# Weight rows of a graph layer: unrelated columns summed from adjacency bytes, and two of eight head additions through GpSimd

## The reference

```python
h = relu(layernorm(x))
q = (h[sub] @ Wq.T + bq), k = (h[obj] @ Wk.T + bk)      # 8 heads of 64, 10000 pairs (sub, obj) below 1500
scores[:, sub, obj] = (q * k).sum(-1) / 8               # elsewhere 0
scores = where(adj, scores, -inf); scores[:, i, i] = 1e-7
x = x + (softmax(scores, axis=2).sum(heads) / 8) @ h
```

## Time and profile before

| what | value |
|---|---|
| median of 3 runs | 1131.22 us (1126.92 to 1132.14) |
| profiled execution | 1126.64 us, its span 1124.9 us |
| PE, DVE, ACT, POOL busy | 1050.8, 917.9, 786.5, 277.0 us |
| L743, float32 products of W with h | 384 records, 184.9 us |
| L1185, additions of a head | 96, 170.8 us, 1.779 each |
| L1196, masks | 96, 161.1 us, 1.715 each |

### The profile page before, as it was taken

The page is one execution under the profiler, slowest core; times in us unless marked ns, Lnnn a source line. Parts: engine busy times, 40 slices in busy tenths (PEclk is TensorE's granted clock), DMA queues, the critical chain, the costliest instruction groups (busy, mean ns, idle before and its releaser), DMA issues. The chain is left out here.

```text
span 1124.9 us, 25112 instructions
## 1 busy us (share of the span) xinstructions
PE 1050.8 (93%) x10560; PEld 715.8 (64%) x10565; DVE 917.9 (82%) x1259; ACT 786.5 (70%) x833; POOL 277.0 (25%) x272
## 2 busy tenths in 40 slices
PE   1999997999999999999988599999999999999997
PEld 1444443444444444444444499999999999999743
DVE  2355146899999999999981899999999999999466
ACT  1244336777777777776633799999999999998122
POOL 2778750000000000000000244334344344434000
PEclk9999998999999999999999799999999999999999
DMA  9640443322212221100054587767777777777311
GB/s 336 162 29 2 114 91 77 79 68 68 66 40 41 68 59 59 38 20 29 23 215 155 156 196 186 183 171 180 183 187 183 191 203 180 181 182 184 122 69 75
DMA packets 71552, 136.45 MB, mean 121 GB/s; under 512 B 9237, under 2 KB 18834, under 8 KB 69394
## 3 DMA queue, kind: packets, MB, share of 16 engines
q1 hardware_dynamic: 50386, 101.19, 25.7%
q0 software_dynamic: 21056, 33.67, 20.4%
HBM read 92.92 MB, written 25.04 MB: 105 GB/s over the span
## 5 line engine op out<-in xcount | busy, mean ns | idle before, releaser
L1511 ACT ACTIVATE area_h<-area_a,keep 128x2048 fp8e4<-128x2048 f32 x197 | 376.8, 1989 | 4.2 <-PE psum L1666 4.1
L1665 PE MATMUL psum<-s_V,area_h 128*128 128x99 bf16 x3072 | 298.1, 209 | 0.8 <-DVE area_b L1437 0.5
L1665 PEld LDWEIGHTS psum<-s_V,area_h 128*128 128x128 fp8e4 x3072 | 283.4, 98 | 1.1 <-DVE area_h L1561 0.7
L1666 PE MATMUL psum<-s_V,area_b 128*128 128x99 bf16 x2048 | 204.1, 209 | 0.0
L1666 PEld LDWEIGHTS psum<-s_V,area_b 128*128 128x128 fp8e4 x2048 | 189.5, 97 | 0.0
L743 PE MATMUL psum<-area_h,f_region 128*128 128x512 f32 x384 | 184.9, 596 | 0.0
L1185 DVE SCALAR_TENSOR_TENSOR f_region<-area_b,s_r,f_region 128x1500 f32<-128x1500 f32 x96 | 170.8, 1779 | 2.2
L1561 DVE TENSOR_TENSOR area_h<-area_h,area_a 128x512 uint32<-128x512 uint32 x256 | 167.9, 686 | 4.4
L1196 DVE CUSTOM_DVE_ANT_0 area_b<-psum,late 128x1500 f32<-128x1500 f32 x96 | 161.1, 1715 | 8.2 <-PE psum L658 8.1
L1668 PE MATMUL psum<-s_V,area_h 128*128 128x198 bf16 x1024 | 150.0, 249 | 13.7 <-DVE area_h L1561 13.7
L977 ACT ACTIVATE area_b<-area_b,s_negm 128x1500 f32<-128x1500 f32 x96 | 147.8, 1540 | 20.9 <-DVE s_negm L1196 19.9
(11 more groups left out here) (185 smaller groups left out, 1423.0 us busy)
## 6 DMA issues: line engine op xcount, KB each, us to landing
area_a<-s_rows SPq DMA_DIRECT2D x16, 1024.0 KB, 7.2
late<-area_h POOLq DMA_DIRECT2D x64, 256.0 KB, 4.4
late<-far_rows SPq DMA_DIRECT2D x60, 256.0 KB, 4.1
area_b<-area_h POOLq DMA_DIRECT2D x48, 256.0 KB, 4.6
area_b<-far_rows SPq DMA_DIRECT2D x45, 256.0 KB, 3.5
rel_planes<-f_h SPq DMA_DIRECT2D x3, 2304.0 KB, 15.9
late<-rel_planes SPq DMA_DIRECT2D x36, 192.0 KB, 2.6
area_h<-in_x SPq DMA_DIRECT2D x4, 1024.0 KB, 12.9
```

Of the source, the lines that this page charges most:

```text
L1511: act.activation(masks[:, j, :], s1b[:, b, :], ACT.Relu, bias=t["s2"][:, n, 0, j:j + 1], scale=BIG, saturate=False).then_inc(signs, 1)
L1665: pe.matmul(out[:, :, 0:DZ], masks[:, j, cols], V[:, b, j, :, 0:DZ], **first)
L1666: last = pe.matmul(out[:, :, DZ:CZ], fars[FAR.index(j)][:, cols], V[:, b, j, :, DZ:CZ], **then)
```

## The change

In short: for related row tiles the columns of the four unrelated tiles (1536 to 2047) no longer go through W. W has 1536 columns; its aggregation has six rounds of two tiles for eight. The sum over the four far tiles is made by PE as in `gather`, from a transposed chunk of adjacency bytes (`far_chunk`, reloaded from DRAM by SP, `load_far`) and kept bf16 parts, twelve products of 512 columns (`sum_far`, `unrelated`). VectorE scales that sum late, with half of c0 as bytes are 2, while adding it to x (`finish_far`). It shares PSUM bank 7 with the sum of W, so the first product of W waits for `finish_far`.

Second, heads 5 and 7 of tiles 0 to 10 are no longer added to W by VectorE. ScalarE scales their exponentials by the ratio of the two heads' factors (`weigh`), GpSimd adds them to heads 4 and 6 (`merge`), and VectorE adds heads 4 and 6 when that is done. The last tile adds all eight.

To make room, small tables of the first stage lie in another buffer, the projected rows have one store buffer for two, and the marked relations lie in their own plane, for which its reload waits longer.

The core of the diff:

```diff
+MERGED = ((4, 5), (6, 7))
@@ bank_rounds
-        order += turns(n, 5) + [quarter[2]] + turns(n, 6) + [quarter[3]] + turns(n, 7) + [("h", n + 2)]
+        order += turns(n, 5) + [quarter[2], quarter[3], ("h", n + 2)]
@@ stage2, SP
+            def load_far(i):
+                k = NU - 1 + i
+                sp.wait_ge(chunk_out[place(k)], 16 * (stored(k) + 1))
+                if i:
+                    sp.wait_ge(far_in, 16 * i)
+                if i >= 2:
+                    sp.wait_ge(far_summed, i - 1)
...
+                sp.dma_start(f.far_chunk[i % 2], t["adj_chunks"][tile_at(k)][:, ET * P:].rearrange("p (j i) -> p j i", j=4)
+                             ).then_inc(far_in, 16)
@@ POOL
+            def merge(n, i):
+                into, source = MERGED[i]
+                pool.wait_ge(weighed, len(MERGED) * n + i + 1)
+                pool.wait_ge(added, added_until(n, 2 * (i + 1)))
+                pool.tensor_tensor(ex[:, into, 0:NREL], ex[:, into, 0:NREL], ex[:, source, 0:NREL], ALU.add).then_inc(merged, 1)
@@ PE
+            def sum_far(i, bank, alone):
+                pe.wait_ge(far_in, 16 * (i + 1))
...
+                for b in range(NT - ET):
+                    moving = (f.upper(h[:, ET + b, :]), f.far_rest[b // 2][:, b % 2, :], f.far_tail[b])
+                    for part in range(3):
...
+                        last = pe.matmul(ps[:, bank, :], f.far_chunk[i % 2][:, b, :], moving[part],
+                                         start=alone and first, stop=alone and final)
+                last.then_inc(far_summed, 1)
@@ aggregate
-                if m == order[0] and r < ET - 1:
-                    pe.wait_ge(*((summed, NU + r) if r else (based, NU)))
+                if m == 0 and blocks[0] == 0 and r < ET - 2:
+                    pe.wait_ge(based, NU + r + 1)
@@ step (PE)
                 if scored:
                     score(n + 1, 0)
+                if turned:
+                    unrelated(r)
                 project(n + 1)
@@ ACT
             def start_w(r):
...
+                act.activation(half[:, r % 2:r % 2 + 1], cd[:, 0:1], ACT.Copy, scale=1.0 / NEAR).then_inc(w_started, 1)
+                act.activation(W[r % 2][:, :], adjn[:, (r + NU) % ADJ_RING, 0:NE], ACT.Copy, scale=cd[:, 0:1]).then_inc(w_started, 1)
+            def weigh(r):
+                act.wait_ge(fac, LINKS * (r + 1))
+                for i, (_, source) in enumerate(MERGED):
+                    act.activation(ex[:, source, 0:NREL], ex[:, source, 0:NREL], ACT.Copy, scale=ratio[:, i:i + 1]).then_inc(weighed, 1)
@@ step (ACT)
                 start_w(n)
+                weigh(n)
@@ DVE
+            def finish_far(r):
+                k = r + NU
+                dve.wait_ge(far_summed, r + 2)
...
+                dve.scalar_tensor_tensor(xt[k % 3][:, :], ps[:, far_bank(r), :], half[:, r % 2:r % 2 + 1], xt[k % 3][:, :],
+                                         ALU.mult, ALU.add).then_inc(based, 1)
@@ factors
+                dve.tensor_tensor(ratio[:, :], z[:, 4:HA:2], rz[:, 5:HA:2], ALU.mult).then_inc(fac, 1)
@@ step (DVE)
                 for p in range(PAIRS):
                     for hd in (2 * p, 2 * p + 1):
-                        add_head(n, hd)
+                        if hd in adds(n):
+                            add_head(n, hd)
+                    if p == 0 and n:
+                        finish_far(n - 1)
                     for hd in (2 * p, 2 * p + 1):
                         if n + 1 < ET:
                             mask(n + 1, hd)
```

More of the change, by code:

```diff
@@ L493, in stage2 @@
     cd = sb("cd", [P, 2])
+    half = sb("half", [P, 2])
+    ratio = sb("ratio", [P, len(MERGED)])
     stats = sb("stats", [P, 6])
@@ L500, in stage2 @@
     chunk_out = [sem(f"chunk_out{i}") for i in range(3)]
-    seq_out = [sem(f"seq_out{i}") for i in range(2)]
+    seq_out = sem("seq_out")
     wseq_in, a_in = sem("wseq_in"), sem("a_in")
@@ L526, in stored, with adds, added_until, far_bank @@
         return sum(place(x) == place(k) for x in ORDER[:ORDER.index(k)])
+    def adds(r):
+        return tuple(hd for hd in range(HA) if r == ET - 1 or hd not in [source for _, source in MERGED])
+    def added_until(r, count):
+        return sum(len(adds(x)) - 1 for x in range(r)) + count
+    def far_bank(r):
+        return 7 if r < ET - 2 else r - ET + 3
     def turned_round(r, m):
@@ L639, in _ @@
             pool.wait_ge(f.rel_in[0], 16 * PLANES)
-            for k in range(NU + 3, NT):
+            for k in range(NU + 3, NU + ADJ_RING):
                 load_adj(k)
-            pool.wait_ge(w_started, ET)
+            for n in range(ET - 1):
+                if n + NU + ADJ_RING < NT:
+                    load_adj(n + NU + ADJ_RING)
+                merge(n, 0)
+                merge(n, 1)
+            pool.wait_ge(w_started, 2 * ET)
             heads.gpsimd(pool)
@@ L743, in aggregate @@
                     last = pe.matmul(ps[:, 7 if r < ET - 1 else 0, :], WT[m % 2][:, b, :], h[:, 2 * m + b, :],
-                                     start=(m == order[0] and b == 0), stop=(m == order[-1] and b == 1))
+                                     start=(m == 0 and b == 0), stop=(m == AG - 1 and b == 1))
                 if blocks[-1] == 1:
@@ L865, in last_steps @@
                 turn_one_and_scores(ET - 1)
-                for m in range(2, 7):
+                for m in range(2, AG):
                     turn_w(r, m)
@@ L1111, in _, with keep_parts @@
         def _(dve):
+            def keep_parts():
+                dve.wait_ge(f.proj, GROUPS)
+                dve.wait_ge(f.parted, 2 * NT)
+                for i in range(2):
+                    upper = f.rest[:, ET + 2 * i:ET + 2 * i + 2, :].bitcast(BF16).rearrange("p t (c w) -> p t c w", w=2)[:, :, :, 1]
+                    dve.tensor_copy(f.far_rest[i], upper).then_inc(f.parted, 1)
+                dve.tensor_copy(f.far_tails, f.tail[:, ET:ET + 2, :]).then_inc(f.parted, 1)
+                for b in (2, 3):
+                    dve.tensor_copy(f.far_tail[b], f.tail[:, ET + b, :]).then_inc(f.parted, 1)
             def score_weights():
@@ L1183, in add_head @@
                 w = W[r % 2][:, 0:NREL]
-                dve.wait_ge(*((added, (HA - 1) * r + hd) if hd else (diag_added, r + 1)))
+                dve.wait_ge(*((added, added_until(r, adds(r).index(hd))) if hd else (diag_added, r + 1)))
+                for i, (into, source) in enumerate(MERGED):
+                    if hd == into and source not in adds(r):
+                        dve.wait_ge(merged, len(MERGED) * r + i + 1)
                 dve.scalar_tensor_tensor(w, ex[:, hd, 0:NREL], r8[:, hd:hd + 1], w, ALU.mult, ALU.add
-                                         ).then_inc(added if hd < HA - 1 else w_ready, 1)
+                                         ).then_inc(added if hd < adds(r)[-1] else w_ready, 1)
             def mask(r, hd):
```

197 lines of the change are left out of this document (111 added, 86 removed).

## The result

The changed kernel takes 1140.75 us (median of four runs, 1139.75 to 1142.16) against 1129.17 us before in the same series: a ratio of 1.0098, 95% interval 1.0067 to 1.0129. Forecast were 1140.6. The profiled execution took 1141.06 us, its span is 1139.3.

A forecast was written before the change was run, and what follows sets the result against it. VectorE's own list was taken as the bound, with TensorE and ScalarE arriving just in time. Eight steps +11.0, three others +2.4 and the tail -4.0 gave +9.4 us on 1131.22: 1140.6, 8-in-10 range 1119 to 1149.

The forecast's parts named there:

- The bound of the kernel before: First-layer step of 33.43 us: VectorE's own list bounds, 6.8 us a pair, just hiding the mask-score loop of 6.23.
- The meeting of three lists at T + 11.1: T is a step's start on VectorE; far correction, ScalarE's projection eviction and TensorE's work meet there, where TensorE stood at 8.51.
- What follows from it: Later pairs of scores come late, VectorE waits ahead of masks, and a step takes 34.8 us against 33.43.
- Two pairs give 0.56 each: VectorE's places with one addition left: each saves 0.56 us and not 1.76, as the 6.23 loop stands.
- GpSimd's additions: Additions of 128x1500 beside masks, taken as 3.7 us each: hidden, nothing in the sum, at most 0.5 us a step.
- The sum: Eight full steps +11.0, the other three overlapping steps +2.4, the tail -4.0: together +9.4 us.
- the tail: TensorE's list behind the overlapping steps: four rounds less, -7.7, two far sums more, +5.3, partly in a wait: -4.0 us.
- The start of the kernel: Five copies on VectorE at the stage's start lie in its 23.9 us idle: nothing, at most 6.0 us once.
- The first (lists decide): Rival: TensorE's list bounds the step, 31.8 us, giving 1110 us in all; chance 0.12.
- The second (the engines catch up, a step of 33.4 to 33.9): Rival: an added wait overlaps, so ScalarE and TensorE catch up; net -4 to +2, about 1130 us; chance 0.15.
- The third (masks held up): Rival: GpSimd holds up masks, +3.0 us a step, 1174 us; chance 0.10 including any other GpSimd or queue hold-up.

The follow-up runs named there:

- Shortening TensorE's list alone: The changed kernel with ten of the twelve far products left out: 1160.37 us in one run.
- VectorE's and ScalarE's lists together: The changed kernel with the far correction between the first two additions and ScalarE's low row behind the projection's eviction: 1135.27 us, ratio 1.0034 to before.
- all three: The changed kernel with far correction early, ScalarE's low row behind the eviction, and ten of twelve far products left out: 1123.76 us in one run.
- late scalings: The changed kernel with ScalarE's scaling of heads 5 and 7 moved behind its eviction of the next tile's projection: 1148.72 us, ratio 1.0144 to before.
- added wait: The rebalanced order plus one GpSimd wait, so its first addition runs beside VectorE's additions, not masks: 1175.86 us in one run.
- second profile of before: The kernel before, unchanged, profiled once more: 1132.03 us in one run.
- rebalanced order: The changed kernel with far correction early, low row late, and TensorE work ahead of the second pair of scores moved behind it: 1126.35 us, ratio 0.9949 to before.

## Why the prediction was right, point by point

- **The bound of the kernel before.** Held. Its rule that a mask starts 2.82 behind its scores gives 393.46 from 390.64 in after, and the row has 393.45.
- **The meeting of three lists at T + 11.1.** Held. The first product of W at T + 10.27 and the turn behind it at T + 11.23 (forecast 10.2, 11.15). Shortening TensorE's list alone gave nothing, moving ScalarE's scalings made it worse (they held something else), VectorE's and ScalarE's lists together gave 0.5 us, all three 1.46. VectorE's alone was not tried.
- **What follows from it.** Second, third and fourth pair of scores at T + 15.46, 22.42 and 28.66, forecast 15.5, 22.5 and 28.7; the masks' waits 1.28, 1.90 and 1.18, forecast 1.3, 2.0 and 1.2; the step 34.76 for 34.8. One sentence there is wrong and doesn't enter the sum: "Two pairs give 0.56 each". Of the two places with one addition less, the first gave nothing, as TensorE's own list stands between the second and third pair of scores (6.97 us, by the prediction's own row), and the second gave 0.63.
- **GpSimd's additions.** 3.37 us, taken as 3.7. The Trainium skill's figure ("GPSIMD Engine Reference", section "Performance versus the Vector engine") had given an estimate of 3.3 and was nearer. Masks kept 1.72, and in this step nothing was held up: the third addition starts 0.33 us behind GpSimd's end (388.58 against 388.25). The forecast had the same 0.3 from a GpSimd addition that began 0.2 earlier and took 0.3 longer, two errors that cancel. That the margin held is luck more than design; the runs with the late scalings and with the added wait show what lay beside it.
- **The sum.** Eleven steps +13.8 (forecast +13.4), the tail -4.1 (forecast -4.0). The parts fit less well than the whole. The eight steps from the third on grew by 1.33 each, the first by 0.58, the last by 0.63, and the second by 1.94: TensorE still has far products (L776) at its beginning, and its first scores come at T + 1.81 for 1.02. And against the second profile of before the tail is -5.8, so a match to 0.1 is luck.
- **The start of the kernel.** I had all of it at nothing, and the profile had +4.8 there. The second profile of before moved by 4.6 at the first joining and by 3.8 at the first step, so most of this is ordinary spread, not a term; the last 1.0 stays open. By the profiled time (1141.06) the forecast for that execution, 1136.0, was 5 too low, which is this. The forecast of the median stands on 1131.22 for before, and the 39 runs of before in the four series have their median at 1131.18 (from 1126.7 to 1136.2): a difference of 9.6 for the forecast's 9.4. In the series of the result itself before had 1129.17 from four runs and the difference is 11.6, so that the two medians agree within 0.2 us is partly luck; that the kernel is 8 to 12 us slower is not.
- **Rivals.** The first (lists decide) needed the second pair by T + 13, which only the rebalanced order comes near, and there the step is 33.07, bound by masks and scores, not 31.8. The second (the engines catch up, a step of 33.4 to 33.9) is false: 34.76. The third (masks held up) is false for masks and true for additions.
- **What I had missed altogether** is the clock: four of the variants lost 1.2 to 3.4 us to it in some or all of their steps, one of them by leaving work out. In after it stayed at 1.00 from the second step on, as in before.

## What to carry to other kernels

Offloading work from the fuller engines gains nothing, or loses as here, when the order puts new work ahead of the item that others wait for: find that item (here the second pair of scores), list what every engine must have done before it, and move all else behind it. When several lists end within tenths of a microsecond, shortening one may do nothing; treat them together. And an engine's shortened list is only worth as much as the wait loop around it: of VectorE's two places with one addition less (1.76 us freed in each), one gave 0.63 us and the other nothing.

## What the runs showed of the hardware

- **VectorE and GpSimd additions exclude each other, masks don't.** Beside a GpSimd addition (3.36 us then) a mask, with one operand in PSUM, takes 1.72 as always; a VectorE addition with both operands in SBUF took up to 3.87 in one kernel and 4.77 in another, for 1.78, and GpSimd's own 4.72. The Trainium skill's page "SBUF — State Buffer", section "SBUF: two separate sides", calls this a lock for a whole instruction, taken by whichever starts first; the rows agree in both directions. In the rebalanced kernel an addition that begins 0.33 us ahead of the recorded end of GpSimd's (383.44, 383.77) is 0.14 longer, so even there a little is lost.
- **TensorE's clock follows its pauses, but not by their length alone.** From the second of the eleven steps on, the kernels whose longest wait on TensorE was 1.6 us or less (before, after, the scalings behind the eviction, both with lists early, the rebalanced ones without the added wait) kept 1.00. A wait of 2.16 us ahead of a step's scores was followed by a fall in every second step, one of 2.48 us in six of ten steps, waits of 3.31 in every step, and waits of 3.1 in every step but one, which had 3.18 and kept 1.00. A kernel busy 30.0 of 33.3 us, with short pauses only, kept 1.00, where one busy 32.0 of 35.2 did not. So the share of a step does not tell it; what exactly decides stays open.
- **Before itself spreads by 9 us** over its 39 runs; between its two profiles 4.6 lie ahead of the first joining, in the wait for the load behind the scatters (13.93 and 17.89 us). The rest was not separated.
